# Row sums and mixes of two tiles side by side, in a fused conditional mix and dequantized linear layer on one core

## What is computed

```python
y = einsum('bct,bcd->bdt', x, W[condition])             # 64x64 mix per sample
w = (unpacked.astype(float32) - zero_point) * scale      # 1024x1024, from 6-bit fields, scale and zero per row n
out = x + einsum('bsk,nk->bsn', y, w) + bias
```

## Time and profile before

| | |
|---|---|
| median of 3 runs | 309.73 us (307.82 to 311.16) |
| profiled execution, its own time | 310.09 us |
| its span, first to last instruction | 307.9 us |
| mean granted TensorE clock | 0.983 of full speed |
| TensorE matmuls, weight loads | 293.3 us (95%), 243.0 us (79%) |
| VectorE, ScalarE, GpSimd | 207.7, 79.1, 78.3 us busy |
| median landing of an x load, a store, a weight block | 3.3, 2.0, 1.9 us |

### The profile page before, as it was taken

The page is one execution under the profiler, slowest core; times in us unless marked ns, Lnnn a source line. Parts: engine busy times, 40 slices in busy tenths (PEclk is TensorE's granted clock), DMA queues, the critical chain, the costliest instruction groups (busy, mean ns, idle before and its releaser), DMA issues.

```text
span 307.9 us, 8409 instructions
## 1 busy us (share of the span) xinstructions
PE 293.3 (95%) x3236; PEld 243.0 (79%) x3236; DVE 207.7 (67%) x261; ACT 79.1 (26%) x169; POOL 78.3 (25%) x39
## 2 busy tenths in 40 slices
PE   8695599999999999999999999999999999999995
PEld 3584478888888888888888888888888888888885
DVE  3569985666666777666666776666666776667554
ACT  3664125222112222222112222221122222210000
POOL 1008305432113333332123333321133333321000
PEclk9989599999999999999999999999999999999999
DMA  6992065544333333244343332343343311110221
GB/s 221 285 375 99 3 209 188 173 146 142 119 131 140 106 137 115 98 140 140 106 140 126 118 136 87 128 140 117 130 140 106 138 71 68 68 70 34 84 89 68
DMA packets 20689, 39.54 MB, mean 128 GB/s; under 512 B 6850, under 2 KB 7106, under 8 KB 20674
## 3 DMA queue, kind: packets, MB, share of 16 engines
q1 hardware_dynamic: 20674, 39.33, 36.8%
HBM read 22.54 MB, written 16.78 MB: 128 GB/s over the span
## 4 chain that ended last, share of the span: by engine, by line
PE 90%; DVE 5%; SPq 1%; DMA 1%; issue 1%; DVEq 0%
PE o_ps L286 77%; PE y_ps L249 11%; DMA q_raw<-in_L_ffn_qweight_dram 1%; PE ysum_ps L263 1%; DVE q_int L422 1%; DVE q_int L420 1%; DVE q_int L424 1%; DVE q_bf L429 1%; PE y_ps L286 1%; PE o_ps L271 1%; DVE y_lo L437 0%; SPq L145 0%; SPq L141 0%; SPq L136 0%; SPq L174 0%
## 5 line engine op out<-in xcount | busy, mean ns | idle before, releaser
L286 PE MATMUL o_ps<-qT,y_hi 128*128 128x512 f32 (+1 forms) x512 | 203.7, 399 | 0.0
L286 PE MATMUL o_ps<-qT,y_lo 128*128 128x512 f32 (+1 forms) x512 | 200.1, 392 | 0.0
L542 POOL TENSOR_TENSOR resid<-x_sb,bias_bc 128x1024 f32<-128x1024 f32 x32 | 77.2, 2415 | 198.9 <-DVE o_sb L465 176.8
L286 PEld LDWEIGHTS o_ps<-qT,y_hi 128*128 128x128 f32 x512 | 97.0, 190 | 21.6
L286 PEld LDWEIGHTS o_ps<-qT,y_lo 128*128 128x128 f32 x512 | 97.1, 190 | 19.7
L457 DVE TENSOR_TENSOR o_sb<-o_ps,scale_bc 128x512 f32<-128x512 f32 x63 | 43.5, 691 | 71.6 <-PE o_ps L286 69.7
L360 ACT ACTIVATE y_hi<-y_ps 128x512 fp32r<-128x512 f32 x64 | 34.8, 596 | 181.4 <-PE y_ps L249 181.4
L446 DVE SCALAR_TENSOR_TENSOR resid<-zs_bc,ysum,resid 128x1024 f32<-128x1024 f32 x32 | 60.0, 1874 | 0.0
L437 DVE TENSOR_TENSOR y_lo<-y_ps,y_hi 128x512 fp32r<-128x512 f32 x64 | 41.2, 686 | 13.6 <-ACT y_hi L360 13.6
L465 DVE TENSOR_TENSOR o_sb<-o_sb,resid 128x512 f32<-128x512 f32 x63 | 43.6, 692 | 2.7 <-DVE resid L446 0.5
L249 PE MATMUL y_ps<-w_sb,x_sb 64*64 64x64 f32 x2048 | 37.8, 223 | 0.3 <-DMA w_sb<-in_L_cond_weights_dram 0.3
(11 more groups left out here) (25 smaller groups left out, 39.7 us busy)
## 6 DMA issues: line engine op xcount, KB each, us to landing
x_sb<-in_x_dram SPq DMA_DIRECT2D x32, 512.0 KB, 3.3
out_dram<-o_sb SPq DMA_DIRECT2D x63, 256.0 KB, 2.0
q_raw<-in_L_ffn_qweight_dram SPq DMA_DIRECT2D x8, 384.0 KB, 5.4
w_sb<-in_L_cond_weights_dram SPq DMA_DIRECT2D x64, 16.0 KB, 1.9
scale_bc<-_L_ffn_weight_scale_dram SPq DMA_DIRECT2D x1, 512.0 KB, 6.7
zs_bc<-n_weight_zero_point_dram SPq DMA_DIRECT2D x1, 512.0 KB, 7.5
bias_bc<-in_L_ffn_bias_dram SPq DMA_DIRECT2D x1, 512.0 KB, 8.3
out_dram<-o_sb SPq DMA_DIRECT2D x2, 128.0 KB, 1.9
```

What stands on the lines that cost most here:

```text
L286: last = nc.tensor.matmul(bank, part[:, slot, kt, :], qT[:, kt, col:col + width], start=(kt == 0 and part is y_hi), stop=(kt == KT - 1 and ...
L542: nc.gpsimd.tensor_tensor(resid[:, j % RING, :], x_sb[:, j % RING, :], bias_bc[:], ALU.add).then_inc(xbias_ready, 1)
```

## The change

`LEAD` becomes 2 and the steps take a pair of tiles, (0, 1) or (2, 3) of the four slots. TensorE's step waits for the inputs of t+2 and t+3, runs both row sums, then both mixes, then the four linear halves of t and t+1. ScalarE makes the copies of both, then both `ysum`, then two row sums of x. VectorE takes four differences, then residual and output of t and of t+1. SyncE issues two loads and then four stores. `sum_y` now waits for `ysum` of the tile four before (the slot of the ring) instead of the one before; `junk`, where `sum_x` writes what nobody reads, gets two slots. In the start-up tile 6 is no longer mixed after tile 2; it becomes the first of the loop's first pair.

```diff
-    LEAD = 3
+    LEAD = 2
+    PAIRS = [(j, j + 1) for j in range(0, RING, 2)]
...
# SyncE
-            def step(j, i, loads=True):
+            def step(pair, i, loads=True):
                 if loads:
-                    reload(j + LOADLEAD, i)
-                for h in range(H):
-                    store(j, i, h)
-
-            step(3, 0)
+                    for j in pair:
+                        reload(j + LOADLEAD, i)
+                for j in pair:
+                    for h in range(H):
+                        store(j, i, h)
+
+            for h in range(H):
+                store(3, 0, h)
             with sp.Fori(1, TRIPS - 2) as i:
-                for j in range(RING):
-                    step(j, i)
...
+                for pair in PAIRS:
+                    step(pair, i)
...
# TensorE
-                if not isinstance(t, int) or t >= 1:
-                    pe.wait_ge(ysum_ready, t)
+                if not isinstance(t, int) or t >= RING:
+                    pe.wait_ge(ysum_ready, t - RING + 1)
...
-            def step(j, i, mixes=True):
+            def step(pair, i, mixes=True):
                 if mixes:
-                    wait_mix(j + LEAD, i)
-                    sum_y(j + LEAD, i)
-                    mix(j + LEAD, i)
-                for h in range(H):
-                    linear(j, i, h)
+                    for j in pair:
+                        wait_mix(j + LEAD, i)
+                    for j in pair:
+                        sum_y(j + LEAD, i)
+                    for j in pair:
+                        mix(j + LEAD, i)
+                for j in pair:
+                    for h in range(H):
+                        linear(j, i, h)
...
             for j in range(3):
                 linear(j, 0, 1)
-                wait_mix(j + RING, 0)
-                mix(j + RING, 0)
-                sum_y(j + RING, 0)
+                if j < LEAD:
+                    wait_mix(j + RING, 0)
+                    mix(j + RING, 0)
+                    sum_y(j + RING, 0)
...
# ScalarE
-            def step(j, i, highs=True, sums=True):
-                if highs:
+            def step(pair, i, sums=True):
+                for j in pair:
                     high(j + LEAD, i)
+                for j in pair:
                     copy_ysum(j + LEAD, i)
                 if sums:
-                    sum_x(j + LEAD + 1, i)
+                    for j in pair:
+                        sum_x(j + 2 * LEAD, i)
...
# VectorE
-            def step(j, i, lows=True):
+            def step(pair, i, lows=True):
                 if lows:
-                    low(j + LEAD, i)
-                residual(j, i)
-                for h in range(H):
-                    finish(j, i, h)
+                    for j in pair:
+                        low(j + LEAD, i)
+                for j in pair:
+                    residual(j, i)
+                    for h in range(H):
+                        finish(j, i, h)
```

More of the change, by code:

```diff
@@ L78, in adaln_ffn @@
         warm = sb("warm", [P, 512], BF16)
-        junk = sb("junk", [P, K], BF16)
+        junk = sb("junk", [P, 2, K], BF16)
         resid = sb("resid", [P, RING, N], F32)
@@ L200, in _ @@
             load_w(3, 0)
[L203 to L208, removed]
-            def step(j, i, loads=True):
-                if loads:
-                    reload(j + LOADLEAD, i)
-                for h in range(H):
-                    store(j, i, h)
-            step(3, 0)
-            with sp.Fori(1, TRIPS - 2) as i:
-                for j in range(RING):
-                    step(j, i)
-            for t in range(TILES - 2 * RING, TILES - 1):
-                step(t % RING, t // RING, loads=t + LOADLEAD < TILES)
+            reload(4, 0)
+            store(0, 0, 0)
+            reload(5, 0)
+            store(1, 0, 0)
+            reload(6, 0)
+            store(2, 0, 0)
+            store(0, 0, 1)
+            reload(7, 0)
+            store(1, 0, 1)
+            reload(8, 0)
+            store(2, 0, 1)
+            reload(9, 0)
+            def step(pair, i, loads=True):
+                if loads:
+                    for j in pair:
[5 more added lines that the diff above has]
+                store(3, 0, h)
+            with sp.Fori(1, TRIPS - 2) as i:
+                for pair in PAIRS:
+                    step(pair, i)
+            step(PAIRS[0], TRIPS - 2)
+            step(PAIRS[1], TRIPS - 2, loads=False)
+            step(PAIRS[0], TRIPS - 1, loads=False)
+            for h in range(H):
+                store(2, TRIPS - 1, h)
             store_last()
@@ L334, in _ @@
             with pe.Fori(1, TRIPS - 1) as i:
[L335 to L338, removed]
+                for pair in PAIRS:
+                    step(pair, i)
+            step(PAIRS[0], TRIPS - 1)
+            for h in range(H):
+                linear(RING - 2, TRIPS - 1, h)
             linear(RING - 1, TRIPS - 1, 0)
@@ L350, in sum_x @@
                     act.wait_ge(ysum_ps_ready, i * RING + j - RING + 1)
[L351 removed]
+                nc.scalar.activation(junk[:, j % 2, :], x_sb[:, j % RING, :], ACT.Copy,
                                      accum_out=xsum[:, j % RING:j % RING + 1]).then_inc(xsum_ready, 1)
@@ L394, in _ @@
             sum_x(4, 0)
-            def step(j, i, highs=True, sums=True):
-                if highs:
+            def step(pair, i, sums=True):
+                for j in pair:
                     high(j + LEAD, i)
+                for j in pair:
                     copy_ysum(j + LEAD, i)
                 if sums:
-                    sum_x(j + LEAD + 1, i)
-            for j in range(1, RING):
-                step(j, 0)
+                    for j in pair:
+                        sum_x(j + 2 * LEAD, i)
+            high(4, 0)
+            copy_ysum(4, 0)
+            sum_x(5, 0)
+            high(5, 0)
+            copy_ysum(5, 0)
+            for t in range(6, 8):
+                sum_x(t, 0)
             with act.Fori(1, TRIPS - 1) as i:
-                for j in range(RING):
-                    step(j, i)
-            step(0, TRIPS - 1, sums=False)
+                for pair in PAIRS:
+                    step(pair, i)
+            step(PAIRS[0], TRIPS - 1, sums=False)
         @block.vector
@@ L497, in _ @@
                 finish(j, 0, 1)
-                low(j + RING, 0)
+                if j < LEAD:
+                    low(j + RING, 0)
             residual(3, 0)
@@ L501, in _ @@
                 finish(3, 0, h)
-            def step(j, i, lows=True):
+            def step(pair, i, lows=True):
                 if lows:
-                    low(j + LEAD, i)
-                residual(j, i)
-                for h in range(H):
-                    finish(j, i, h)
-            with dve.Fori(1, TRIPS - 1) as i:
[L511 to L514, removed]
+                    for j in pair:
+                        low(j + LEAD, i)
+                for j in pair:
+                    residual(j, i)
+                    for h in range(H):
+                        finish(j, i, h)
+            with dve.Fori(1, TRIPS - 1) as i:
+                for pair in PAIRS:
+                    step(pair, i)
+            step(PAIRS[0], TRIPS - 1)
+            residual(2, TRIPS - 1)
+            for h in range(H):
+                finish(2, TRIPS - 1, h)
             residual(RING - 1, TRIPS - 1)
```

## The result

The changed kernel took 305.8 us (median of 4, 305.56 to 306.89), the kernel before in the same comparison 309.44 us. The ratio is 0.9873, interval 0.9831 to 0.9915: 3.9 us less. Run again beside other versions it came to 305.2 us and 0.9828 (0.9792 to 0.9863). So it is faster, by 1.3 to 1.7%. The forecast was 305.5 us. Each of these is the time of a whole execution, start-up included; single executions of the changed kernel went from 303.2 to 306.9 us.

What follows compares the result with a forecast made beforehand. The prediction took TensorE's unbroken stream of work as the bound. Small work falling from 38.4 to 34.2 us saves 4.2 us from the profiled 310.09, and 0.36 less for the median gives 305.5 us, range 303.2 to 308.7.

Steps and rivals of the forecast that it cites:

- Step 1: TensorE's second mix of a pair costs its 64 starts, 0.94 us, and saves 0.32 us a pair.
- Step 2: TensorE's second row sum of a pair costs two uncovered weight loads, 0.22 us, +0.01 us a pair against today.
- both bounds: Limits for the second row sum: nothing if both loads ran beside the first sum, 0.41 us at most.
- Steps 3 and 4: TensorE's small work falls from 2.95 to 2.63 us a pair; over 13 pairs 38.4 becomes 34.2, saving 4.2 us.
- Step 6: VectorE's four differences and 2.00 us residual before emptying the first bank stay hidden, with 2.5 us of cover.
- Steps 5, 7, 8 and 9: The end is unchanged, ScalarE's two sums and SyncE's queue stay hidden, and the start-up has no new wait.
- step 8: SyncE's queue: two loads through about 8 us after the first mix's start, first store 0.4 us late, hidden.
- The rule against a row: Skill's 25 ns least start distance would make the second mix 1.6 us, 314 us in all; the trace's 0.94 was used.
- Full loads: Rival: the second row sum on TensorE pays 0.41 us instead of 0.22, giving 308.0 us; chance 0.13.
- Clock: Rival: TensorE's clock falls in the small matmuls, 1.5 us a pair, giving 325 us; chance 0.04.
- Nothing saved: Rival: the stream shortens but the kernel waits elsewhere, on VectorE or a transfer, 309 to 310 us; chance 0.08.
- The slow feed: Rival: instructions fall behind in the second mix, starts 65 to 128, 0.78 us more, giving 315.7 us; chance 0.05.

Runs made afterwards that it cites:

- sum, mix, sum, mix: Changed kernel with TensorE's order in a pair sum, mix, sum, mix instead of sum, sum, mix, mix; 309.65 us, 0.9967 of the kernel before.
- the six operations: Changed kernel with six more VectorE operations in each pair, between the differences and the first residual; 313.69 us, 1.0098 of the kernel before.
- The one by one version: Changed kernel with its lead of two and start-up, but every engine takes tiles one by one again; 310.91 us, 0.9998 of the kernel before.
- rows of 256: Changed kernel with each mix in the loop run twice, so 256 small matmuls in a row; 334.84 us, 1.0777 of the kernel before.

## Why the prediction was right, step by step

- *The time.* 305.5 us was forecast, 305.8 and 305.2 were measured. That it came this close is partly luck: the loop gave 0.5 us more than the sum, and the start-up moves by more than that. What is confirmed is the saving, about 4 to 5 us, and where it comes from.
- *The bound.* Right: TensorE's stream set the time before and sets it after, with no wait in the loop in either trace.
- *Step 1, the second mix.* Predicted 0.94 us; 128 matmuls and the way out take 2.02 us, for 2.03 predicted, and mixes run twice cost 0.935 us each. Run between two mixes, the second sum brings the way out back.
- *Step 2, the second sum.* Predicted 0.22, measured 0.22 (0.43 for two sums less 0.21; sums run twice: 0.22). The start-up's loads behind a mix were the right neighbour, and both bounds were far off.
- *Steps 3 and 4.* Predicted 0.32 us a pair, measured 0.36. The term that was off is the re-entry: I had kept 0.06 us a pair for starts a little apart behind the second linear matmul, and only about 0.03 us of it is left (from 152.16 to 166.80 it is 14.64 us; 64 linear matmuls at 0.2265 us make 14.50, the first step 0.11 more). The length of the row of mixes is not the cause: with sum, mix, sum, mix the row ahead of the linear matmuls is 64 long, and the same stretch is 14.65 us (152.55 to 167.20). What is no run shows. With 13 pairs the loop gives 4.7 us instead of 4.2; 3.9 and 5.3 us were measured; 4.7 lies in both intervals (2.6 to 5.2 and 4.3 to 6.5 us), 4.2 only in the first.
- *Step 6, VectorE.* Right in place. The bank is empty 6.8 us behind the first mix's start (156.92) where 6.9 was forecast, and TensorE is back at it after 9.4 us (159.55), as forecast. The size that was off is the residual, 1.28 us instead of 2.00: VectorE is early and waits 0.57 us for the bank's data, and this idle time is cover too. So there are 3.2 us of it by this trace, and 3.0 by the six operations, instead of 2.5.
- *Steps 5, 7, 8 and 9.* TensorE waits for none of this in the loop. In step 8 a size was off: the two loads held SyncE's queue until 158.63, 8.5 us behind the first mix's start instead of 8, and the pair's first store, ready at 157.64, went out at 158.82, 1.2 us late instead of 0.4; it stayed hidden. The one by one version shows that the start-up's part is nothing that the times can tell.
- *The rule against a row.* The Trainium skill's least distance of 25 ns between matmul starts ("TensorE: Matmul & The Clock Gate", Wait — 56ns, not 53.3ns?) fails here in every mix, whose matmuls go to the four quarters of the array in turn: 128 start in 1.9 us, 0.015 us apart.
- *The rivals.* Full loads: out, by sums run twice. Clock: out, the granted clock is 1.00 from 64 to 280 us. Nothing saved: out, both intervals end below 1 (0.9915 and 0.9863). The slow feed was given 0.05, for the right reason against it (no slowing within a mix) but with a price from another cause, the lower clock. Where instructions did come late, with rows of 256, it was in gaps of 1.3 to 1.8 us in code that runs for the first time, three of them, and not in every pair. The chances of the cases add up to 0.30 for no clear change and 0.09 for slower, where 0.29 and 0.10 were given.

## What to carry to other kernels

Where the trace has one engine without a gap, price a reordering by the distances between its starts, form of instruction by form: what a change of form costs on the way in and out, what of a weight load is covered by the instruction before. Put short work of one form together until it needs a resource that is not there (here PSUM has room for two mixed tiles), and count the cover of the engines that must then serve two at once. Compare loops by their period in the trace; the whole time carries a start-up that moved here by 1.6 us between two executions of one kernel, a third of the gain, while the period was the same to 0.01 us.

## What the runs showed that was not expected

*VectorE and GpSimd slow each other, and the one that comes second pays.* The page's groups for the residual and the add, after the change (mean ns of one behind the busy time):

```profile
L472 DVE SCALAR_TENSOR_TENSOR resid<-zs_bc,ysum,resid 128x1024 f32<-128x1024 f32 x32 | 40.9, 1277 | 0.0
L573 POOL TENSOR_TENSOR resid<-x_sb,bias_bc 128x1024 f32<-128x1024 f32 x32 | 88.7, 2776 | 182.9 <-DVE o_sb L491 160.1 <-DMA bias_bc<-in_L_ffn_bias_dram 22.9
```

On the page of before the residual's mean was 1874 ns and the add's 2415. Before, the add started at 153.40, ahead of the residual of 154.89, which then took 2.00 us, and the add 2.40. After, GpSimd's timeline reads

```profile
151.47 2.40 POOL L573 TENSOR_TENSOR resid<-x_sb,bias_bc 128x1024 f32<-128x1024 f32 x1 [3.94 <-DVE o_sb L491]
161.31 3.31 POOL L573 TENSOR_TENSOR resid<-x_sb,bias_bc 128x1024 f32<-128x1024 f32 x1 [7.44 <-DVE o_sb L491]
```

The first add of a pair runs beside the differences, which read one of their two inputs from PSUM, and costs 2.40 us; the second starts at 161.31, behind the residual of 161.09, which keeps its 1.28 us, and takes 3.31. Where this add is still under way at VectorE's next sum of two inputs in SBUF (`add_residual`, L491, at 164.10), that one takes 1.07 us instead of 0.69; the emptying of a bank (L483, at 163.38), with one input in PSUM, keeps its 0.69. The Trainium skill has this in "SBUF — State Buffer" (SBUF: two separate sides): VectorE with two inputs in SBUF and a GpSimd operation that reads SBUF share a pair of ports under an exclusive lock, and who starts first keeps it for the whole instruction. The trace agrees in both orders, though each of the two waited a little less than what was left of the other: the residual of before 0.72 us of 0.91, the add after the change 0.91 of 1.06. It cost nothing here, since TensorE waits for neither.

*TensorE can run dry* without any semaphore: three gaps of 1.34 to 1.80 us in rows of 256 small matmuls, in the first two pairs of the loop and in the last behind it, none in the later passes.
